# Fewer row-sum matmuls in the attention of a transformer layer: one running sum per head on the diagonal, both heads' maxima turned together, and a VectorE addition that joins two partial sums off the diagonal

## The chip, the cores and the metric

The kernel runs on one core of a Trainium2 chip. The metric is the time of one execution on the device in microseconds (us). The engines' names in the profile are PE (TensorE's matmuls), PEld (TensorE's weight loads), DVE (VectorE), ACT (ScalarE), POOL (GpSimd) and SP (SyncE, which issues transfers).

## The reference

One layer computes a layer norm, causal attention with 16 heads of 32 over 2048 tokens, and a gated feed-forward block, all in float32. Cut to what matters here:

```python
scores = jnp.einsum('bhqd,bhkd->bhqk', q, k) * scale
scores = jnp.where(causal, scores, jnp.finfo(scores.dtype).min)
probs = jax.nn.softmax(scores, axis=-1)
attn = jnp.einsum('bhqk,bhkd->bhqd', probs, v)
...
x = x + attn_out + ffn_out      # ffn: dequantised gate, up and down weights, tanh gelu
```

## The kernel before

Three stages follow one another: norm and projection (until about 160 us), attention (160 to 757 us), and output projection with feed-forward (757 us to the end). The change is in attention alone.

Attention goes through the 16 heads in 8 **pairs**. A pair has 40 **steps**: a step is one chunk of 512 queries against one tile of 128 keys. Four steps make a **group**, so a pair has 10 groups and the kernel has 80 (`NG`), with the index `k`. A group is **diagonal** if its keys are those of its own queries, and **full** otherwise; over the ten groups of a pair the order is D F D F F D F F F D (0 to 9), which makes 32 diagonal and 48 full groups. Each engine has its own program, and counting semaphores join them.

What each engine does for a group:

- **PE** computes the scores with keys on the partitions (`scores_t`, four steps ahead; with `mask_t` on the diagonal), and 8 **units** of scores with queries on the partitions (`scores`, line 772), which are used only for the row maxima and run up to 56 units ahead. It puts row maxima through a turning matmul (`turn_max`), multiplies exponentials and values (`product_v`, line 825), and adds up the exponentials over the keys with a matmul against a column of ones (`row_sums`, line 837). `row_sums(k)` of a diagonal group stands right behind its own products; that of a full group stands in the next group, behind seven of that group's eight units and ahead of its products. The eighth unit comes last in the group.
- **DVE** takes the maximum of each unit (`unit_max`, lines 697 and 701) in order. The units share a ring of four banks (`S_BUFS`), in which a turning also takes a slot.
- **ACT** takes the exponentials (line 638) into a ring of 16 tiles, `e_sb`, and copies turned maxima to `q_stack`.
- **POOL** adds exponentials in pairs of steps into `e_sum` (line 570), a ring of 6 tiles: four additions a group, two per head, each of two tiles. It also splits the row maxima into three parts (`split`) and multiplies the output of the pair before by its reciprocals (`normalise`, line 602, four times a pair).

The four matmuls of a quartet in `product_v` and `row_sums` write to four different quarters of the partitions (two heads, two halves of the queries), and their records overlap in time. A float32 matmul leaves two records, a bfloat16 or float32r matmul one.

DVE's loop over groups takes the units of a group with `for n in units: unit_max(n)`. The last units belong to group 72; groups 73 to 79 have none.

Of the kernel before, what the change touches and what calls it, by code (L numbers as in the profile page):

```python
# [292 lines left out]
def attention(nc, qk_scratch, v_scratch, sum_scratch, rsum_scratch, wo_t, wo_sb, attn_t, xn_hi, xn_lo, e_sb, wv_hi, wv_lo, p_v,  # L293
# [7 lines left out]
    HALF = W // 2  # L301
    SUMS = 4
    SUM_BUFS = 6
# [45 lines left out]
    for p in range(PAIRS):  # L349
        for r in range(TC):  # L350
            last = p * NU + UNITS_TO[r]
            BATCHES[-1 if last <= FIRST else next(k for k in range(NG) if unit_end[k] >= last)].append((p, r))
            wanted = (p * NS + CHUNK_START[r] - LEAD) // GS
            for a in range(2):
                TURNS[max(-1, -1 if p == 0 and r < 2 else wanted - TURN_LEAD)].append((p, r, a))
    turn_index = {}
# [12 lines left out]

    def summed(k, m):  # L370
        g = GS * k + 2 * (m // 2)
        q0, q1 = STEPS[g % NS][2], STEPS[(g + 1) % NS][2]
        return g * PIECES + m % 2, (g + 1) * PIECES + m % 2, q1 - q0, W - q1

    pool_sums = {(k, m): SUMS * k + m + 1 for k in range(NG) for m in range(SUMS)}

# [4 lines left out]
    with ExitStack() as ctx:  # L381
# [19 lines left out]
        rest2 = sb("rest2", [P, 2, TT], F32)  # L401
        max_cols = sb("max_cols", [P, 2, TT, D], BF16)
        ident = sb("ident_bf", [P, P], BF16)
# [25 lines left out]
        exp_done = sem("exp_done")  # L429
        pool_summed = sem("pool_summed")  # L430
        rows_done = sem("rows_done")
        pv_done = sem("pv_done")
# [103 lines left out]
        def _(pool):  # L536
# [22 lines left out]
            def sum_steps(k, part, before):  # L559
                for m in part:  # L560
                    if k < 0 or k >= NG:
                        continue
                    n = SUMS * k + m
                    x, y, skip, w = summed(k, m)
                    pool.wait_ge(exp_done, y + 1)
                    if before:
                        pool.wait_ge(normalised, before)
                    if n >= SUM_BUFS:
                        pool.wait_ge(rows_done, (n - SUM_BUFS) // SUMS + 1)
                    nc.gpsimd.tensor_tensor(e_sum[:, n % SUM_BUFS, 0:w], e_sb[:, x % E_BUFS, skip:skip + w],  # L570
                                            e_sb[:, y % E_BUFS, 0:w], ALU.add).then_inc(pool_summed, 1)

            def split(p, r, before):

                n = p * TC + r
                tiles = slice(4 * r, 4 * r + 4)
                pool.wait_ge(row_maxed, n + 1)
                if before:
                    pool.wait_ge(normalised, before)
                if p:  # L580
                    pool.wait_ge(max_turned, turn_index[p - 1, r, 1] + 1)
                nc.gpsimd.tensor_copy(max_cols[:, :, tiles, 0], row_max[:, :, tiles]).then_inc(split_step, 1)
                pool.wait_ge(split_step, 4 * n + 1)
                nc.gpsimd.tensor_tensor(rest1[:, :, tiles], row_max[:, :, tiles], max_cols[:, :, tiles, 0],
                                        ALU.subtract).then_inc(split_step, 1)
                pool.wait_ge(split_step, 4 * n + 2)
                nc.gpsimd.tensor_copy(max_cols[:, :, tiles, 1], rest1[:, :, tiles]).then_inc(split_step, 1)
                pool.wait_ge(split_step, 4 * n + 3)
                nc.gpsimd.tensor_tensor(rest2[:, :, tiles], rest1[:, :, tiles], max_cols[:, :, tiles, 1],
                                        ALU.subtract).then_inc(split_step, 1)  # L590
                pool.wait_ge(split_step, 4 * n + 4)
                nc.gpsimd.tensor_copy(max_cols[:, :, tiles, 2], rest2[:, :, tiles]).then_inc(max_split, 1)

# [12 lines left out]
            for k in range(-1, NG):  # L606
                sum_steps(k, (2, 3), products)
# [3 lines left out]
                sum_steps(k + 1, (0, 1), products)  # L611
                p, s = divmod(GS * k, NS)
                if p > 0 and s in (24, 28, 32, 36):
                    normalise(p - 1, products % TC, splits, pool_sums[min((k + 1, 1), (NG - 1, SUMS - 1))])
                    products += 1

        @block.scalar
        def _(act):
            def max_row(p, r, a):
                act.wait_ge(max_turned, turn_index[p, r, a] + 1)  # L620
                nc.scalar.activation(q_stack[p % PB][a][ROWS:P, r * W:(r + 1) * W],
                                     p_s[ROWS:P, slot[p, r, a] % S_BUFS, :], ACT.Copy).then_inc(max_rows, 1)

            def exps(x):
# [5 lines left out]
                if x >= E_BUFS:  # L630
                    old = piece(x - E_BUFS)[0]
                    j, i = divmod(old, GS)
                    act.wait_ge(pv_done, old + 1)
                    if DIAG[old % NS] and i % 2 == 0:
                        act.wait_ge(rows_done, j + 1)
                    m = 2 * (i // 2) + (x - E_BUFS) % PIECES
                    act.wait_ge(pool_summed, pool_sums[j, m])
                nc.scalar.activation(e_sb[:, x % E_BUFS, 0:w], bank_st(x)[:, 0:w], ACT.Exp,  # L638
# [46 lines left out]
        def _(dve):  # L685
# [30 lines left out]
            def divide(qc):  # L716
# [13 lines left out]
                for a in range(2):  # L730
                    for h in range(2):
                        rows = slice((2 * a + h) * D, (2 * a + h + 1) * D)
                        nc.vector.tensor_tensor(attn_rows(p, a, qc)[:, h * HALF:(h + 1) * HALF], o[rows, 0, :],
                                                recip[rows, 0:HALF], ALU.mult).then_inc(divided, 1)

            for n in range(FIRST):
                unit_max(n)
                for p, r in BATCHES[-1]:
                    if n + 1 == UNITS_TO[r]:
                        join_parts(p, r)  # L740
            for k in range(NG):
                p, s = divmod(GS * k, NS)
                if p and s == 16:
                    invert_sums(p - 1)
                units = units_of(k)
                for n in units:
                    unit_max(n)
                    for p_, r in BATCHES[k]:
                        if n + 1 == p_ * NU + UNITS_TO[r]:
                            join_parts(p_, r)  # L750
# [5 lines left out]
        def _(pe):  # L756
            def bank_free(n):

                before = ring[n - S_BUFS] if n >= S_BUFS else None
                if before in turn_index:  # L760
                    pe.wait_ge(max_rows, turn_index[before] + 1)
                elif before is not None:
                    pe.wait_ge(maxed, before + 1)
# [11 lines left out]

            def turn_max(p, r, a):

                n = slot[p, r, a]
                pe.wait_ge(max_split, p * TC + r + 1)
                bank_free(n)  # L780
                for t in range(W // P):
                    last = nc.tensor.matmul(p_s[ROWS:P, n % S_BUFS, t * P:(t + 1) * P],
                                            max_cols[:, a, 4 * r + t, :], ident[:, :], start=True, stop=True)
                last.then_inc(max_turned, 1)

            def scores_t(x):
# [6 lines left out]
                if kt == 0:  # L793
                    pe.wait_ge(max_rows, turn_index[p, qc, a] + 1)
                if x >= ST_BUFS:
# [35 lines left out]
            def row_sums(k):  # L831
                p, s = divmod(GS * k, NS)
                pe.wait_ge(pool_summed, pool_sums[k, SUMS - 1])


                def add(a, h, first, end, what, stop):
                    return nc.tensor.matmul(p_o[(2 * a + h) * D:(2 * a + h + 1) * D, 1, first:end], ones[:, :], what,  # L837
                                            start=False, stop=stop)

                if DIAG[s]:  # L840
                    for a in range(2):
                        x, _, _, _ = summed(k, a)
                        add(a, 0, 0, P, e_sb[:, x % E_BUFS, 0:P], False)
                    for a in range(2):
                        n = SUMS * k + a
                        add(a, 0, P, HALF, e_sum[:, n % SUM_BUFS, 0:P], True)
                    for a in range(2):
                        n = SUMS * k + a
                        add(a, 1, 0, HALF, e_sum[:, n % SUM_BUFS, P:3 * P], False)
                    for a in range(2):  # L850
                        x, _, _, _ = summed(k, 2 + a)
                        add(a, 1, 0, P, e_sb[:, x % E_BUFS, 0:P], False)
                    for a in range(2):
                        n = SUMS * k + 2 + a
                        last = add(a, 1, P, HALF, e_sum[:, n % SUM_BUFS, 0:P], True)
                else:
                    for j in range(2):
                        for h in range(2):
                            for a in range(2):
# [460 lines left out]
```

## Time and profile before

| | |
|---|---|
| median of 3 runs | 1872.63 us (1871.89 to 1872.90) |
| the profiled execution's own time | 1872.51 us |
| its span | 1870.6 us |
| PE busy over the span | 1815.5 us, 97% |
| DVE, ACT, POOL busy over the span | 59%, 38%, 37% |
| PE busy in attention, 160 to 757 us | 578.54 us of 597 |
| DVE, ACT, POOL busy in attention | 373.10, 347.56, 397.74 us |

An engine's busy time is the union of its instructions' records. A row of a timeline begins with the start and the duration in us, merges equal neighbours (xcount), and in brackets names the idle time ahead of it and what ended it; of a merged row, start plus duration is the end of the last record. PEclk is the granted clock of TensorE: 1.00 is 2.4 GHz and 0.50 is 1.2 GHz.

### The profile page before, as it was taken

The numbers are of one execution on the slowest core, as the hardware profiler recorded it, in microseconds if no ns is written. First come the engines' busy times: TensorE is split into PE (matmuls) and PEld (weight loads), VectorE is DVE, ScalarE is ACT, GpSimd is POOL, SyncE is SP. The second block draws the span as 40 slices with busy tenths as digits, with TensorE's granted clock in tenths as the row PEclk, the third lists the DMA queues.
The fourth block names the chain that finished last, engine by engine and source line by source line (L and its number), as shares of the span: only waits on it lengthen the run. The fifth ranks groups of instructions, "written<-read, shape, count | busy, mean of one in ns | idle before, by whom it ended". The sixth has DMA issues, their size and how long they took to land.

```text
span 1870.6 us, 29693 instructions
## 1 busy us (share of the span) xinstructions
PE 1815.5 (97%) x10880; PEld 1372.9 (73%) x10880; DVE 1111.8 (59%) x1695; ACT 698.5 (37%) x1144; POOL 702.7 (38%) x674
## 2 busy tenths in 40 slices
PE   6999999999999999899999999999999999999997
PEld 4877666666666664368888888888888888888886
DVE  4514766666666665437756665676666567666642
ACT  2313565665655655013332233232322333223221
POOL 4330567677677677112222222222222222222221
PEclk9999999999999999999999999999999999999999
DMA  7675041341341400521001101100110110010002
GB/s 247 218 213 156 27 89 42 79 89 39 81 89 35 85 8 13 213 68 34 7 28 34 34 0 34 34 13 21 34 34 0 34 34 18 16 34 0 0 1 90
DMA packets 73011, 108.64 MB, mean 58 GB/s; under 512 B 24608, under 2 KB 44688, under 8 KB 69264
## 3 DMA queue, kind: packets, MB, share of 16 engines
q1 hardware_dynamic: 72912, 107.34, 21.0%
q8 instruction: 59, 0.97, 0.2%
q14 instruction: 40, 0.33, 0.1%
HBM read 74.04 MB, written 29.59 MB: 55 GB/s over the span
## 4 chain that ended last, share of the span: by engine, by line
PE 58%; DVE 0%; ACT 0%; POOLq 0%; issue 0%; POOL 0%
PE p_gate L50 6%; PE p_gate L51 6%; PE p_gate L49 6%; PE p_out L49 6%; PE p_out L50 6%; PE p_out L51 6%; PE p_up L50 6%; PE p_up L51 6%; PE p_up L49 6%; PE p_out L1248 1%; PE p_gate L1248 1%; PE p_up L1248 1%; DVE acc L1183 0%; POOLq L939 0%; DVE inter L1163 0%
## 5 line engine op out<-in xcount | busy, mean ns | idle before, releaser
L1107 POOL TENSOR_SCALAR poly<-poly 128x1024 f32<-128x1024 f32 x64 | 71.3, 1113 | 839.5 <-ACT poly L1074 839.5
L570 POOL TENSOR_TENSOR e_sum<-e_sb 128x512 f32<-128x512 f32 (+2 forms) x320 | 331.3, 1063 | 107.5 <-PE p_o L837 103.8
L701 DVE TENSOR_REDUCE max_part<-p_s 128x1 f32<-128x512 f32 x384 | 240.8, 683 | 57.0 <-PE p_s L772 56.4
L638 ACT ACTIVATE e_sb<-p_v 128x512 f32<-128x512 f32 (+3 forms) x427 | 216.3, 552 | 142.4 <-PE p_v L799 76.6
L1163 DVE SCALAR_TENSOR_TENSOR inter<-inter,gate 128x1024 f32<-128x1024 f32 x64 | 78.4, 1225 | 255.2 <-ACT inter L1079 254.5
L772 PE MATMUL p_s<-k_stack,q_stack 96*128 96x512 f32 (+3 forms) x640 | 217.2, 393 | 3.7 <-DMA k_stack<-qk_scratch 3.2
L697 DVE CUSTOM_DVE_ANT_0 recip<-p_s,score_mask 128x128 bf16<-128x128 f32 (+3 forms) x256 | 119.7, 487 | 166.3 <-PE p_s L772 163.9
L49 PE MATMUL p_out<-i_hi,w_hi 128*128 128x512 f32 x512 | 200.0, 391 | 3.1 <-DVE acc L1183 3.1
L50 PE MATMUL p_out<-i_lo,w_hi 128*128 128x512 f32 x512 | 199.7, 390 | 0.0
L51 PE MATMUL p_out<-i_hi,w_lo 128*128 128x512 f32 x512 | 199.7, 390 | 0.0
L49 PE MATMUL p_gate<-xn_hi,w_hi 128*128 128x512 f32 x512 | 199.6, 390 | 0.0
L51 PE MATMUL p_gate<-xn_hi,w_lo 128*128 128x512 f32 x512 | 199.2, 389 | 0.0
L50 PE MATMUL p_gate<-xn_lo,w_hi 128*128 128x512 f32 x512 | 199.2, 389 | 0.0
L49 PE MATMUL p_up<-xn_hi,w_hi 128*128 128x512 f32 x512 | 199.2, 389 | 0.0
L50 PE MATMUL p_up<-xn_lo,w_hi 128*128 128x512 f32 x512 | 199.2, 389 | 0.0
L51 PE MATMUL p_up<-xn_hi,w_lo 128*128 128x512 f32 x512 | 199.2, 389 | 0.0
L1073 ACT ACTIVATE gate<-p_gate 128x1024 f32<-128x1024 f32 x64 | 65.9, 1029 | 355.4 <-PE p_gate L51 355.4
L1110 POOL TENSOR_TENSOR poly<-poly,gate 128x1024 f32<-128x1024 f32 x64 | 178.3, 2785 | 5.3
L799 PE MATMUL p_v<-q_stack,k_stack 128*128 128x512 f32 (+3 forms) x427 | 159.3, 397 | 8.1 <-ACT e_sb L638 5.1
L825 PE MATMUL p_o<-e_sb,v_stack 128*32 128x256 f32 (+1 forms) x2304 | 152.8, 370 | 0.0
L1183 DVE TENSOR_TENSOR acc<-acc,p_out 128x2048 f32<-128x2048 f32 x64 | 145.9, 2280 | 7.4 <-PE p_out L51 7.4
L772 PEld LDWEIGHTS p_s<-k_stack,q_stack 96*128 96x128 f32 x640 | 116.1, 190 | 43.6 <-issue 23.6
(124 smaller groups left out, 3060.6 us busy)
## 6 DMA issues: line engine op xcount, KB each, us to landing
q_stack<-qk_scratch SPq DMA_DIRECT2D x48, 256.0 KB, 7.1
k_stack<-qk_scratch SPq DMA_DIRECT2D x48, 256.0 KB, 8.1
qk_scratch<-out_hi SPq DMA_DIRECT2D x32, 256.0 KB, 2.6
qk_scratch<-out_lo SPq DMA_DIRECT2D x32, 256.0 KB, 3.2
scales<-in_gate_up_s SPq DMA_DIRECT2D x128, 64.0 KB, 2.3
x_sb<-in_x SPq DMA_DIRECT2D x4, 1024.0 KB, 13.2
xn_lo_scratch<-xn_lo SPq DMA_DIRECT2D x4, 1024.0 KB, 5.2
v_scratch<-o_sb SPq DMA_DIRECT2D x16, 256.0 KB, 2.0
```

The costliest lines, as they stand in the source:

```text
L49: nc.tensor.matmul(out, w_hi, x_hi, start=first, stop=False)
L50: nc.tensor.matmul(out, w_hi, x_lo, start=False, stop=False)
L51: return nc.tensor.matmul(out, w_lo, x_hi, start=False, stop=last)
L570: nc.gpsimd.tensor_tensor(e_sum[:, n % SUM_BUFS, 0:w], e_sb[:, x % E_BUFS, skip:skip + w], e_sb[:, y % E_BUFS, 0:w], ALU.add).then_inc(poo ...
L638: nc.scalar.activation(e_sb[:, x % E_BUFS, 0:w], bank_st(x)[:, 0:w], ACT.Exp, scale=SCALE).then_inc(exp_done, 1)
L697: nc.vector.tensor_tensor_reduce(out=masked_scores[:, m % 2, 0:w], in0=p_s[:, slot[n] % S_BUFS, 0:w], in1=score_mask[:, W - w:], scale=1.0 ...
L701: nc.vector.reduce_max(part, p_s[:, slot[n] % S_BUFS, 0:w], AX.X).then_inc(maxed, 1)
L772: nc.tensor.matmul(p_s[:, slot[n] % S_BUFS, 0:w], q_stack[p % PB][a][0:ROWS, i * P:(i + 1) * P], k_stack[p % PB][a][0:ROWS, b * W:b * W + ...
L799: last = nc.tensor.matmul(bank_st(x)[:, 0:W - q0], k_stack[p % PB][a][:, kt * P:(kt + 1) * P], q_stack[p % PB][a][:, qc * W + q0:(qc + 1) ...
L825: last = nc.tensor.matmul(p_o[(2 * a + h) * D:(2 * a + h + 1) * D, 0, first - h * HALF:], v_stack[p % PB][:, kt, a, :], e_sb[:, (g * PIECE ...
L1110: nc.gpsimd.tensor_tensor(poly[:, :, :], poly[:, :, :], gate[:, :, :], ALU.mult).then_inc(poly_done, 1)
L1183: nc.vector.tensor_tensor(here, here, p_out[:, :, :], ALU.add).then_inc(added, 1)
```

## The change

Three things are changed.

1. **Diagonal groups.** Before, POOL made two sums per head (steps 0+1 and 2+3) and PE multiplied ten tiles by ones. Now POOL adds steps 2 and 3 in place to the sum of steps 0+1, so a group has six additions (2 of 384 columns, 2 of 256, 2 of 128) and PE has six matmuls.
2. **Full groups.** POOL's four additions stay. DVE then adds the second sum of a head to the first (`join_sums`, two additions of 128x512 a group), and PE has four matmuls of 256 columns in place of eight. `row_sums` of a full group waits for DVE now (`vector_summed`), no longer for POOL.
3. **Turned maxima.** `max_cols` holds the two heads side by side, and one turning of 64 rows takes the place of two of 32. It takes one slot of the ring; ACT copies both heads out of it with two instructions, as before.

```diff
+    ADDS, first_sum, sums, added = [], [], 0, 0
+    adds_before, sum_group = [], []
+    for k in range(NG):
+        if DIAG[GS * k % NS]:
+            ADDS.append([(a, a, 1, 0) for a in range(2)] + [(a, a, i, None) for i in (2, 3) for a in range(2)])
+        else:
+            ADDS.append([(2 * j + a, a, 2 * j + 1, 2 * j) for j in range(2) for a in range(2)])
...
+                    if x is None:
+                        here = e_sum[:, n % SUM_BUFS, q0 - P:W - P]
+                        pool.wait_ge(pool_summed, adds_before[k] + i - 1)
+                        other = here
...
+            def join_sums(k):
+                if k not in FULL:
+                    return
+                for a in range(2):
+                    one, other = ((first_sum[k] + m) % SUM_BUFS for m in (a, 2 + a))
+                    dve.wait_ge(pool_summed, adds_before[k] + 3 + a)
+                    nc.vector.tensor_tensor(e_sum[:, one, :], e_sum[:, one, :], e_sum[:, other, :],
+                                            ALU.add).then_inc(vector_summed, 1)
...
                 units = units_of(k)
+                if len(units) < 6:
+                    join_sums(k - 1)
                 for n in units:
                     unit_max(n)
+                    if len(units) >= 6 and n == units[5]:
+                        join_sums(k - 1)
...
                 for t in range(W // P):
-                    last = nc.tensor.matmul(p_s[ROWS:P, n % S_BUFS, t * P:(t + 1) * P],
-                                            max_cols[:, a, 4 * r + t, :], ident[:, :], start=True, stop=True)
+                    last = nc.tensor.matmul(p_s[2 * D:P, n % S_BUFS, t * P:(t + 1) * P],
+                                            max_cols[:, 4 * r + t, :, :].rearrange("p a d -> p (a d)"), ident[:, :],
+                                            start=True, stop=True)
...
             def row_sums(k):
                 p, s = divmod(GS * k, NS)
-                pe.wait_ge(pool_summed, pool_sums[k, SUMS - 1])
+                if DIAG[s]:
+                    pe.wait_ge(pool_summed, adds_before[k] + len(ADDS[k]))
+                else:
+                    pe.wait_ge(vector_summed, 2 * FULL.index(k) + 2)
...
-                    for j in range(2):
-                        for h in range(2):
-                            for a in range(2):
-                                n = SUMS * k + 2 * j + a
-                                last = add(a, h, 0, HALF, e_sum[:, n % SUM_BUFS, h * HALF:(h + 1) * HALF], False)
+                    for h in range(2):
+                        for a in range(2):
+                            last = add(a, h, 0, HALF, total(a, h * HALF, (h + 1) * HALF), False)
```

The order on DVE around group 8 of the first pair, before. L697 and L701 are the maxima of units (an `ISA` row of `max_part` alone is the second half of a masked maximum), L708 joins their parts:

```order
L697 ISA recip,max_part<-p_s,score_mask 128x384 [waits maxed,scored]
L697 ISA max_part 128x1
L697 ISA recip,max_part<-p_s,score_mask 128x384 [waits maxed,scored]
L697 ISA max_part 128x1
L701 TENSOR_REDUCE max_part<-p_s 128x1 [waits scored] x4
L697 ISA recip,max_part<-p_s,score_mask 128x512 [waits maxed,scored]
```

The same place in the changed kernel (L722 and L726 are the unit maxima there):

```order
L722 ISA recip,max_part<-p_s,score_mask 128x384 [waits maxed,scored]
L722 ISA max_part 128x1
L722 ISA recip,max_part<-p_s,score_mask 128x384 [waits maxed,scored]
L722 ISA max_part 128x1
L726 TENSOR_REDUCE max_part<-p_s 128x1 [waits scored] x4
L767 TENSOR_TENSOR e_sum<-e_sum 128x512 [waits pool_summed] x2
L722 ISA recip,max_part<-p_s,score_mask 128x512 [waits maxed,scored]
```

The two additions of the group before stand behind the maxima of six units and ahead of those of the seventh and eighth.

The order on PE at the end of the same group, before: seventh unit (L772), two turnings (L782), row sums of the group before (L837), products (L825):

```order
L772 MATMUL p_s<-k_stack,q_stack 128x512 [waits maxed]
L782 MATMUL p_s<-ident_bf,max_cols 32x128 [waits maxed,max_split]
L782 MATMUL p_s<-ident_bf,max_cols 32x128 x3
L782 MATMUL p_s<-ident_bf,max_cols 32x128 [waits maxed,max_split]
L782 MATMUL p_s<-ident_bf,max_cols 32x128 x3
L837 MATMUL p_o<-e_sum,ones 32x256 [waits pool_summed]
L837 MATMUL p_o<-e_sum,ones 32x256 x7
L825 MATMUL p_o<-e_sb,v_stack 32x256 [waits exp_done]
```

The same place on PE in the changed kernel (L810 unit, L820 turning, L879 row sums, L864 products):

```order
L810 MATMUL p_s<-k_stack,q_stack 128x512 [waits maxed]
L820 MATMUL p_s<-ident_bf,max_cols 64x128 [waits maxed,max_split]
L820 MATMUL p_s<-ident_bf,max_cols 64x128 x3
L879 MATMUL p_o<-e_sum,ones 32x256 [waits vector_summed]
L879 MATMUL p_o<-e_sum,ones 32x256 x3
L864 MATMUL p_o<-e_sb,v_stack 32x256 [waits exp_done]
```

Half of the turnings and half of the row sums are gone; the row sums keep their place, and the semaphore ahead of them is another.

## Rows read from the trace of the kernel before

**Rows 1.** Busy time by engine in attention (windows).

```profile
core 0: us, PE busy (x) PEld busy (x) DVE busy (x) ACT busy (x) POOL busy (x), PEclk, DMA share, GB/s
160.00:757.00 597.00, 578.54 (x5559) 372.82 (x5557) 373.10 (x926) 347.56 (x757) 397.74 (x503) 0.99 0.28 61
```

**Rows 2.** Timeline of PE: turnings, row sums of a full group, products.

```profile
399.83 0.59 PE L782 MATMUL p_s<-ident_bf,max_cols 128*32 128x128 bf16 x5
400.21 0.42 PE L837 MATMUL p_o<-e_sum,ones 128*32 128x256 f32 x3
...
401.10 1.26 PE L825 MATMUL p_o<-e_sb,v_stack 128*32 128x256 f32 x17
```

**Rows 3.** Timeline of PE: end of the row sums of diagonal group 30.

```profile
410.06 0.39 PE L837 MATMUL p_o<-e_sb,ones 128*32 128x128 f32 x4
410.28 0.39 PE L837 MATMUL p_o<-e_sum,ones 128*32 128x128 f32 x4
```

**Rows 4.** Timeline of DVE: maxima up to a sixth unit (groups 32, 34, 35, 37, 38, 39).

```profile
418.78 3.68 DVE L701 TENSOR_REDUCE max_part<-p_s 128x1 f32<-128x512 f32 x6 [0.37 <-PE p_s L772]
...
434.59 1.29 DVE L701 TENSOR_REDUCE max_part<-p_s 128x1 f32<-128x512 f32 x2 [0.39 <-PE p_s L772]
...
441.88 1.28 DVE L701 TENSOR_REDUCE max_part<-p_s 128x1 f32<-128x512 f32 x2
...
455.31 1.88 DVE L701 TENSOR_REDUCE max_part<-p_s 128x1 f32<-128x512 f32 x3
...
461.00 2.62 DVE L701 TENSOR_REDUCE max_part<-p_s 128x1 f32<-128x512 f32 x4
...
467.65 3.68 DVE L701 TENSOR_REDUCE max_part<-p_s 128x1 f32<-128x512 f32 x6
```

**Rows 5.** Timeline of PE: start of the row sums in the same six groups.

```profile
421.40 1.07 PE L837 MATMUL p_o<-e_sum,ones 128*32 128x256 f32 x16
...
435.48 0.42 PE L837 MATMUL p_o<-e_sum,ones 128*32 128x256 f32 x3
...
442.26 1.07 PE L837 MATMUL p_o<-e_sum,ones 128*32 128x256 f32 x16
...
455.95 1.07 PE L837 MATMUL p_o<-e_sum,ones 128*32 128x256 f32 x16
...
463.33 0.42 PE L837 MATMUL p_o<-e_sum,ones 128*32 128x256 f32 x3
...
470.90 0.42 PE L837 MATMUL p_o<-e_sum,ones 128*32 128x256 f32 x3
```

**Rows 6.** Groups by form, DVE: an operation of two SBUF operands, 128x512.

```profile
L1139 DVE TENSOR_TENSOR pair<-pair,high 128x512 int32<-128x512 int32 x48 | 33.2, 692 | 1.6
```

**Rows 7.** Line 733: durations min/median/max, first and last start.

```profile
L733 DVE TENSOR_TENSOR acc<-o_sb,recip x12: 419/1383/1541, 710.4 to 735.4; 32x256 f32<-32x256 f32 x12
L733 DVE TENSOR_TENSOR acc<-p_o,recip x4: 416/422/430, 755.3 to 756.7; 32x256 f32<-32x256 f32 x4
```

**Rows 8.** Timeline of POOL: normalise in groups 37 and 39.

```profile
456.29 1.28 POOL L602 TENSOR_TENSOR acc<-acc,rsum_rows 64x512 f32<-64x512 f32 x1 [0.23 <-POOL e_sum L570]
...
471.22 1.28 POOL L602 TENSOR_TENSOR acc<-acc,rsum_rows 64x512 f32<-64x512 f32 x1 [0.23 <-POOL e_sum L570]
```

**Rows 9.** Waits over the span: us in total, times, longest.

```profile
POOL e_sum L570 <- PE p_o L837: 103.8, 43, 7.4
```

**Rows 10.** POOL's additions of 384 columns (lines), the last two of 128 (timeline).

```profile
L570 POOL TENSOR_TENSOR e_sum<-e_sb 128x384 f32<-128x384 f32 x64 | 63.1, 1006 | 0.1
...
751.47 0.86 POOL L570 TENSOR_TENSOR e_sum<-e_sb 128x128 f32<-128x128 f32 x2
```

**Rows 11.** PE and its granted clock in three stretches (windows), one timeline row.

```profile
176.90:180.30 3.40, 2.66 (x19) 1.00 0.40 154
...
740.00:743.50 3.50, 2.67 (x19) 1.00 0.00 0
743.50:746.90 3.40, 3.40 (x36) 0.50 0.00 0
...
743.39 1.85 PE L837 MATMUL p_o<-e_sum,ones 128*32 128x256 f32 x16
```

More of the change, by code:

```diff
@@ L353, in attention @@
             wanted = (p * NS + CHUNK_START[r] - LEAD) // GS
-            for a in range(2):
-                TURNS[max(-1, -1 if p == 0 and r < 2 else wanted - TURN_LEAD)].append((p, r, a))
+            TURNS[max(-1, -1 if p == 0 and r < 2 else wanted - TURN_LEAD)].append((p, r))
     turn_index = {}
@@ L366, in attention, with used_up @@
     slot = {what: n for n, what in enumerate(ring)}
[L370 to L375, printed above, removed]
+    ADDS, first_sum, sums, added = [], [], 0, 0
[5 more added lines that the diff above has]
+            ADDS.append([(2 * j + a, a, 2 * j + 1, 2 * j) for j in range(2) for a in range(2)])
+        first_sum.append(sums)
+        adds_before.append(added)
+        sum_group += [k] * (2 if DIAG[GS * k % NS] else 4)
+        sums = len(sum_group)
+        added += len(ADDS[k])
+    FULL = [k for k in range(NG) if not DIAG[GS * k % NS]]
+    def used_up(g, a):
+        k, i = divmod(g, GS)
+        return adds_before[k] + 1 + max(n for n, (_, b, y, x) in enumerate(ADDS[k]) if b == a and i in (x, y))
     def piece(x):
@@ L430, in attention @@
         pool_summed = sem("pool_summed")
+        vector_summed = sem("vector_summed")
         rows_done = sem("rows_done")
@@ L559, in sum_steps @@
             def sum_steps(k, part, before):
[L560 to L565, printed above, removed]
+                if k < 0 or k >= NG:
+                    return
+                for i, (m, a, y, x) in list(enumerate(ADDS[k]))[part]:
+                    n = first_sum[k] + m
+                    g = GS * k + y
+                    q0 = STEPS[g % NS][2]
+                    here = e_sum[:, n % SUM_BUFS, 0:W - q0]
+                    pool.wait_ge(exp_done, g * PIECES + a + 1)
                     if before:
                         pool.wait_ge(normalised, before)
[L568 to L571, printed above, removed]
+                    if x is None:
[3 more added lines that the diff above has]
+                    else:
+                        if n >= SUM_BUFS:
+                            pool.wait_ge(rows_done, sum_group[n - SUM_BUFS] + 1)
+                        skip = q0 - STEPS[(GS * k + x) % NS][2]
+                        other = e_sb[:, ((GS * k + x) * PIECES + a) % E_BUFS, skip:skip + W - q0]
+                    nc.gpsimd.tensor_tensor(here, other, e_sb[:, (g * PIECES + a) % E_BUFS, 0:W - q0],
+                                            ALU.add).then_inc(pool_summed, 1)
             def split(p, r, before):
@@ L606, in _ @@
             for k in range(-1, NG):
-                sum_steps(k, (2, 3), products)
+                sum_steps(k, slice(2, None), products)
                 for p, r in BATCHES[k]:
@@ L610, in _ @@
                     splits += 1
-                sum_steps(k + 1, (0, 1), products)
+                sum_steps(k + 1, slice(0, 2), products)
                 p, s = divmod(GS * k, NS)
                 if p > 0 and s in (24, 28, 32, 36):
-                    normalise(p - 1, products % TC, splits, pool_sums[min((k + 1, 1), (NG - 1, SUMS - 1))])
+                    normalise(p - 1, products % TC, splits, adds_before[k + 1] + 2 if k + 1 < NG else added)
                     products += 1
@@ L618, in _, with max_row @@
         def _(act):
[L619 to L622, printed above, removed]
+            def max_row(p, r):
+                act.wait_ge(max_turned, turn_index[p, r] + 1)
+                for a in range(2):
+                    nc.scalar.activation(q_stack[p % PB][a][ROWS:P, r * W:(r + 1) * W],
+                                         p_s[(2 + a) * D:(3 + a) * D, slot[p, r] % S_BUFS, :],
+                                         ACT.Copy).then_inc(max_rows, 1)
             def exps(x):
@@ L631, in exps @@
                     old = piece(x - E_BUFS)[0]
-                    j, i = divmod(old, GS)
                     act.wait_ge(pv_done, old + 1)
[L634 to L637, printed above, removed]
+                    act.wait_ge(pool_summed, used_up(old, (x - E_BUFS) % PIECES))
+                    if STEPS[old % NS][1] == 4 * STEPS[old % NS][0]:
+                        act.wait_ge(rows_done, old // GS + 1)
                 nc.scalar.activation(e_sb[:, x % E_BUFS, 0:w], bank_st(x)[:, 0:w], ACT.Exp,
@@ L760, in bank_free @@
                 if before in turn_index:
-                    pe.wait_ge(max_rows, turn_index[before] + 1)
+                    pe.wait_ge(max_rows, 2 * turn_index[before] + 2)
                 elif before is not None:
@@ L774, in scores, with turn_max @@
                                  ).then_inc(scored, 1)
-            def turn_max(p, r, a):
-                n = slot[p, r, a]
+            def turn_max(p, r):
+                n = slot[p, r]
                 pe.wait_ge(max_split, p * TC + r + 1)
@@ L793, in scores_t @@
                 if kt == 0:
[L794 removed]
+                    pe.wait_ge(max_rows, 2 * turn_index[p, qc] + a + 1)
                 if x >= ST_BUFS:
@@ L838, in add, with total @@
                                             start=False, stop=stop)
+                def total(m, first, end):
+                    return e_sum[:, (first_sum[k] + m) % SUM_BUFS, first:end]
                 if DIAG[s]:
                     for a in range(2):
-                        x, _, _, _ = summed(k, a)
-                        add(a, 0, 0, P, e_sb[:, x % E_BUFS, 0:P], False)
+                        add(a, 0, 0, P, e_sb[:, (GS * k * PIECES + a) % E_BUFS, 0:P], False)
                     for a in range(2):
-                        n = SUMS * k + a
-                        add(a, 0, P, HALF, e_sum[:, n % SUM_BUFS, 0:P], True)
+                        add(a, 0, P, HALF, total(a, 0, P), True)
                     for a in range(2):
[L848 to L855, printed above, removed]
-                else:
-                    for j in range(2):
-                        for h in range(2):
-                            for a in range(2):
-                                n = SUMS * k + 2 * j + a
-                                last = add(a, h, 0, HALF, e_sum[:, n % SUM_BUFS, h * HALF:(h + 1) * HALF], False)
+                        last = add(a, 1, 0, HALF, total(a, P, 3 * P), True)
+                else:
+                    for h in range(2):
+                        for a in range(2):
+                            last = add(a, h, 0, HALF, total(a, h * HALF, (h + 1) * HALF), False)
                 last.then_inc(rows_done, 1)
```

21 lines of the change are left out of this document (11 added, 10 removed).

## The prediction

> **What bounds the kernel now.** I read the busy times of attention first. PE is busy for 578.54 of 597 us there, DVE for 373.10 and POOL for 397.74 [rows 1]: PE sets the pace, and on an average over the stage the others have room. That invites the sum "fewer matmuls, less time". But PE runs its program in order, so I then read, group by group, at what moment DVE has finished the sixth unit and at what moment PE reaches the row sums [rows 4, 5]. There is no room at that place: DVE is still behind PE there.
>
> **What the change takes from PE.** Row sums of a full group: eight matmuls take from 400.21 to the first product at 401.10, 0.89 us [rows 2], so four cost 0.445 and 48 groups give 48 x 0.445 = 21.4 us. Diagonal groups: of the second half's matmuls, two sets of 128 columns go; a set takes 410.28 - 410.06 = 0.22 us [rows 3], so 0.44 a group and 32 x 0.44 = 14.1 us. The first half loses nothing. Turnings: eight matmuls start within 0.38 us (399.83 to 400.21) [rows 2]; four fewer save 0.2. This counts only in the one turning of four per pair behind which no full group's row sums stand; in the other three PE only arrives earlier at a wait (below). 8 x 0.2 = 1.6 us. Together 37.1 us.
>
> **What it puts on the path.** PE's row sums of full group k-1 now need both additions on DVE, and these stand in DVE's order behind the sixth unit of group k. The sixth unit ends, in the six groups of one pair that follow a full one, at 422.46, 435.88, 443.16, 456.59, 463.62 and 471.33 (start plus duration; in group 37 the merged row holds the fifth to seventh units, so one unit of 0.60 less) [rows 4]. PE starts the row sums at 421.40, 435.48, 442.26, 455.95, 463.33 and 470.90 [rows 5]. So DVE is 1.06, 0.40, 0.90, 0.64, 0.29 and 0.43 us late before it has added anything, 3.7 us a pair.
>
> The addition itself (128x512 float32, both operands in SBUF) isn't in this trace. The nearest row has the same shape, both operands in SBUF and four bytes an element: 692 ns [rows 6]. Two are 1.38 us. From below, the mean unit maximum costs about 0.61 from start to start (3.68 us for six), so two are at least 1.2; from above see "collisions". I take 1.38 because the row differs only in the operation. The stall is then 3.7 + 6 x 1.38 = 12.0 us a pair.
>
> I count it in full. DVE's chain starts when PE has scored a group's first unit, and it sets when the row sums start; behind them PE still has the products, the eighth unit and the next group's first scores before it can score another first unit. While PE waits, nothing of that gets done, since it is queued behind the waiting matmul. Only PE's savings behind the wait come off, and they are in the 37.1. Seven pairs and group 72 (1.06 + 1.38 = 2.4) make 43 such waits: 7 x 12.0 + 2.4 = 86.4 us. In groups 73 to 79 DVE has no units and joins early, so there I add nothing.
>
> **Collisions of DVE and POOL.** A DVE multiplication of 32x256 takes 422 ns with one operand in PSUM while POOL is idle, and 1383 ns (median) with both in SBUF while POOL adds [rows 7]: DVE waits there until POOL's current instruction has ended. So I looked where POOL is when the joins would start. In groups 37 and 39 it is in a normalisation that ends at 457.57 and 472.50 [rows 8], 0.98 and 1.17 us behind DVE's sixth unit: 2.15 a pair, 7 x 2.15 = 15.0 us. In the other four POOL is mostly idle. Over the span it waits for PE's row sums 43 times, 2.4 us each [rows 9], and the joins fall just ahead of those row sums. Bounds: nothing, and one such wait for each of two additions in all 43 groups, 43 x 2 x (1.383 - 0.422) = 83 us.
> The Trainium skill (SBUF — State Buffer, "SBUF: two separate sides") has a rule against this change: VectorE with two SBUF inputs and GpSimd share a port pair under an exclusive lock, and the one that comes second is blocked for the whole instruction. By it a join that meets POOL pays what is left of POOL's instruction, and every meeting costs; line 733's times agree, and what it doesn't say is how often they meet.
>
> **POOL's extra work.** Two more additions of 256 columns in a diagonal group, each between 0.455 (128 columns, 0.86 for two) and 1.006 us (384) [rows 10], say 0.73: 1.46 a group. They hide under a group of PE (597 us / 80 = 7.5 us), and the diagonal sums no longer need a slot freed by the group before. In group 79 nothing hides them: POOL's last addition ends at 752.33 [rows 10], PE's last row sums stand behind it, and 1.5 us are added. Splitting into another layout and ACT's copies keep their number and size: nothing.
>
> **The clock.** In 740.0 to 743.5 PE was busy for 2.67 of 3.5 us in short pieces, and the next 3.4 us ran at 0.50, that is at 1.2 GHz [rows 11]. Eight row-sum matmuls took 1.85 us there against 1.07 in group 37 [rows 5, 11], 0.78 more; a stretch of 3.4 us at half speed loses at most 1.7. Against it: with 2.66 of 3.4 us busy at 176.9 the clock stood at 1.00 [rows 11], and over the whole stage it is 0.99 [rows 1]. The new waits are 2 us on average and in one piece, more idle time than either case. I take a fall behind half of the 43 waits at 1.2 us, midway: 26 us. Bounds: none, and 43 x 1.7 = 73 us.
> The Trainium skill (TensorE: Matmul & The Clock Gate, "HAM oscillation") tells of kernels in which every wait is followed by a cold start. By that rule the term would be its upper bound, and the time 1938 + 73 = 2011 us.
>
> **The sum**, against the profiled execution's 1872.5 us (0.1 below the median of the runs shown): -37.1 + 86.4 + 15.0 + 1.5 = +65.8 gives 1938.3; with the clock's 26 it is 1964.
>
> **The rivals.**
>
> - *The waits come, the clock holds*: 1922 without any collision (1872.5 - 37.1 + 86.4) to 1938 with those above. For it: the full clock at 176.9. Chance 0.30.
> - *The clock falls behind every wait, or POOL meets every join*: 2011, or 1922 + 83 + 1.5 = 2006. For it: the waits are long, and line 733 shows how dear a meeting is. Against it: POOL's 43 idle times. Chance 0.14.
> - *The other side: the joins hide* and PE keeps its saving: 1872.5 - 37.1 + 1.5 = 1837. It takes two finished additions when PE arrives, that is DVE earlier by 1.67 to 2.44 us in each group (lateness plus 1.38). It would happen if DVE could start units earlier than now; each of the six chains starts when PE scores its first unit, so I see no way. It decides from the point where the stall per pair is under 37.1/7.2 = 5.2 us in place of 12.0. Chance 0.05.
> - *Saving and waits cancel*, within 0.2% (3.7 us): the stall a pair would have to be half of what I read. Chance 0.02.
>
> **How the numbers follow.** My forecast (waits, some collisions, clock falling behind some of the waits; 1940 to 2000) has 0.49 and is centred on 1964. The range must hold 8 in 10: 1914 (the first rival's low end with additions at 1.2 a pair of them, 43 x 0.18 = 7.7 less) to 2008 (the second rival's two prices). What a measurement of this kernel can tell from no change is about 0.2%. Faster by more: 0.05; within: 0.02; slower by more: 0.93.
>
> **What would show it.** In the new profile PE idles ahead of the row sums, released by DVE's `e_sum` additions, 43 times by about 2 us, and attention is longer by 40 us at least, while the stages around it keep their times. Six units and two additions stand on DVE without a gap ahead of each such release. The additions take about 0.69 us, 1 us more where they meet POOL. PEclk within attention shows falls to 0.50 if the last term is right. PE's busy time falls by some 37 us if the clock holds. I'm wrong if the additions start ahead of the sixth unit's end, or if PE's waits are shorter than 1 us; then the saving shows.

## The result, and the profile after

The changed kernel takes 1998.8 us (median of 4 runs, 1996.29 to 2001.54) against 1872.26 us: 1.0678 times the time of before, 95% interval 1.0662 to 1.0693. The profiled execution took 1996.29 us, 123.8 more than that of before. The forecast was 1964 with a range of 1914 to 2008.

First the stretches. Windows of the changed kernel, attention and what follows it (busy time of each engine, granted clock):

```profile
160.00:885.00 725.00, 604.31 (x4785) 360.42 (x4784) 457.00 (x1016) 350.13 (x754) 449.67 (x567) 0.90 0.22 50
885.00:1994.50 1109.50, 1099.48 (x4732) 889.14 (x4730) 678.01 (x648) 309.09 (x304) 249.58 (x128) 1.00 0.11 33
```

All of the loss is in attention: it ends at about 881 us, not 757, and the rest of the program takes as long as before. PE's busy share there fell from 97% [rows 1] to 83%, and its mean granted clock from 0.99 to 0.90. PE has fewer matmuls and yet more busy time (604 us against 578.54), because some of them ran at half speed.

Then the waits over the whole span (us in total, times, longest):

```profile
PE p_o L879 <- DVE e_sum L767: 102.2, 46, 3.3
POOL e_sum L593 <- PE p_o L879: 61.5, 24, 5.2
```

L879 are the row sums, L767 is the new addition. PE waits 46 times, 2.2 us each; the wait didn't exist before. POOL waits for PE's row sums for 61.5 us in place of 103.8 [rows 9].

The new addition's line (durations in ns, minimum, median, maximum):

```profile
L767 DVE TENSOR_TENSOR e_sum<-e_sum x96: 677/682/1790, 206.8 to 869.8; 128x512 f32<-128x512 f32 x96
```

The timeline of group 37, the one that stood in [rows 4, 5, 8]. DVE:

```profile
505.95 0.42 DVE L722 CUSTOM_DVE_ANT_0 recip<-p_s,score_mask 128x256 bf16<-128x256 f32 x1
506.29 1.28 DVE L726 TENSOR_REDUCE max_part<-p_s 128x1 f32<-128x512 f32 x2
507.49 2.20 DVE L767 TENSOR_TENSOR e_sum<-e_sum 128x512 f32<-128x512 f32 x2
509.62 0.68 DVE L726 TENSOR_REDUCE max_part<-p_s 128x1 f32<-128x512 f32 x1
514.12 0.69 DVE L726 TENSOR_REDUCE max_part<-p_s 128x1 f32<-128x512 f32 x1 [3.82 <-PE p_s L810]
```

PE and POOL in the same group:

```profile
506.60 0.39 PE L838 MATMUL p_st<-q_stack,k_stack 128*128 128x512 f32 x1
509.75 1.08 PE L879 MATMUL p_o<-e_sum,ones 128*32 128x256 f32 x8 [2.76 <-DVE e_sum L767]
510.60 3.05 PE L864 MATMUL p_o<-e_sb,v_stack 128*32 128x256 f32 x32
...
507.29 1.26 POOL L627 TENSOR_TENSOR acc<-acc,rsum_rows 64x512 f32<-64x512 f32 x1 [0.23 <-POOL e_sum L593]
```

Read it in this order. DVE runs six units without a gap and then the two additions; they take 2.20 us in place of 1.28, because the first meets POOL's normalisation, which ends at 508.55. PE has nothing left to do from about 507.0 and starts its row sums at 509.75, right behind the additions. Then its products take 3.05 us for 32 records: at full speed they took 1.91 (456.84 to 458.75 in the trace of before). The windows of PE say why:

```profile
507.00:510.40 3.40, 0.65 (x8) 0.87 0.00 0
509.50:512.90 3.40, 3.15 (x32) 0.50 0.00 0
512.90:516.00 3.10, 3.10 (x29) 1.00 0.00 0
```

Behind the wait the clock is granted at 0.50 (1.2 GHz), and the products run in that stretch.

Not every wait is followed by such a fall. In group 27, the same place one pair earlier, PE waited almost as long, and its products ran at full speed (timeline of PE):

```profile
422.67 0.64 PE L879 MATMUL p_o<-e_sum,ones 128*32 128x256 f32 x8 [2.58 <-DVE e_sum L767]
423.13 1.91 PE L864 MATMUL p_o<-e_sb,v_stack 128*32 128x256 f32 x32
```

By the timeline of PE and its windows, the clock was at 0.50 over part of what followed in 36 of the 46 waits; behind the other ten the products took the full-speed 1.91 us for 32 records, or 1.70 for 24.

### The profile page after: what moved, and what is told of

Read it like the earlier page. It is cut to its first block, busy times and chain, and to the rows that moved or that the text cites. A ratio compares the mean times of both kernels' runs of the same rounds, so it can differ in the third digit from the quotient of the medians.

```text
span 1994.5 us, 28287 instructions
## 1 busy us (share of the span) xinstructions
PE 1840.8 (92%) x10112; PEld 1361.4 (68%) x10112; DVE 1197.7 (60%) x1791; ACT 701.8 (35%) x1144; POOL 754.7 (38%) x738
## 4 chain that ended last, share of the span: by engine, by line
PE 55%; DVE 0%; ACT 0%; POOLq 0%; issue 0%; POOL 0%
PE p_gate L49 6%; PE p_gate L51 6%; PE p_gate L50 6%; PE p_out L49 6%; PE p_out L50 6%; PE p_out L51 6%; PE p_up L49 6%; PE p_up L50 6%; PE p_up L51 6%; PE p_out L1282 1%; PE p_gate L1282 1%; PE p_up L1282 1%; DVE acc L1217 0%; POOLq L973 0%; DVE inter L1197 0%
## 5 line engine op out<-in xcount | busy, mean ns | idle before, releaser
L593 POOL TENSOR_TENSOR e_sum<-e_sb 128x512 f32<-128x512 f32 (+1 forms) x256 | 306.5, 1225 | 75.3 <-PE p_o L879 61.5
L726 DVE TENSOR_REDUCE max_part<-p_s 128x1 f32<-128x512 f32 x384 | 241.2, 682 | 69.5 <-PE p_s L810 69.0
L722 DVE CUSTOM_DVE_ANT_0 recip<-p_s,score_mask 128x128 bf16<-128x128 f32 (+3 forms) x256 | 119.5, 486 | 200.6 <-PE p_s L810 198.1
L810 PE MATMUL p_s<-k_stack,q_stack 96*128 96x512 f32 (+3 forms) x640 | 219.9, 397 | 1.0 <-DMA k_stack<-qk_scratch 0.4
L864 PE MATMUL p_o<-e_sb,v_stack 128*32 128x256 f32 (+1 forms) x2304 | 189.4, 441 | 0.0
L879 PE MATMUL p_o<-e_sum,ones 128*32 128x256 f32 (+1 forms) x640 | 82.6, 470 | 102.2 <-DVE e_sum L767 102.2
L663 ACT ACTIVATE e_sb<-p_st 128x512 f32<-128x512 f32 (+2 forms) x213 | 117.6, 552 | 116.5 <-PE p_st L838 72.9
```

What stands on the lines that cost most here:

```text
L593: nc.gpsimd.tensor_tensor(here, other, e_sb[:, (g * PIECES + a) % E_BUFS, 0:W - q0], ALU.add).then_inc(pool_summed, 1)
L722: nc.vector.tensor_tensor_reduce(out=masked_scores[:, m % 2, 0:w], in0=p_s[:, slot[n] % S_BUFS, 0:w], in1=score_mask[:, W - w:], scale=1.0 ...
L726: nc.vector.reduce_max(part, p_s[:, slot[n] % S_BUFS, 0:w], AX.X).then_inc(maxed, 1)
L810: nc.tensor.matmul(p_s[:, slot[n] % S_BUFS, 0:w], q_stack[p % PB][a][0:ROWS, i * P:(i + 1) * P], k_stack[p % PB][a][0:ROWS, b * W:b * W + ...
L864: last = nc.tensor.matmul(p_o[(2 * a + h) * D:(2 * a + h + 1) * D, 0, first - h * HALF:], v_stack[p % PB][:, kt, a, :], e_sb[:, (g * PIECE ...
```

## The experiments

The kernel before was measured beside each set of these kernels, at 1871.6 to 1872.0 us. Group and pair are those of the front part.

**One change taken out: no joining on DVE.** Full groups have their eight row-sum matmuls again; diagonal sums and joint turning stay.

```diff
-                    pe.wait_ge(vector_summed, 2 * FULL.index(k) + 2)
+                    pe.wait_ge(pool_summed, adds_before[k] + len(ADDS[k]))
...
-                if len(units) < 6:
-                    join_sums(k - 1)
```

> The diagonal sums and the joint turning alone: full groups keep their four POOL sums and eight row-sum matmuls of before, and DVE joins nothing. My theory, by which the cost comes from PE waiting for DVE's additions: 1872.3 less 14.1 us (diagonal row sums) and less 32 x 0.2 = 6.4 us (turnings, which all count now), plus 1.5 us at the end: about 1853 us, and PEclk in attention back at 0.99. The rival, by which POOL's two extra additions in a diagonal group or the changed ring of sums slow the kernel: above 1872 us, with PE waiting for POOL's e_sum in diagonal groups.

Measured: 1863.25 us, ratio 0.9958 (0.9944 to 0.9972). The loss is gone, and the sign of the theory holds: the joining, with the four row-sum matmuls a group that it saves, turns 1863 into 1999. But the gain is 8.6 us, not 19. Waits of this kernel:

```profile
PE p_o L875 <- POOL e_sum L593: 13.1, 8, 3.2
```

Six of these waits stand at the end of a pair, 8.9 us together, where PE needs POOL's in-place additions. They are those of the second to the seventh pair; at the end of the first, which has no normalisations, PE doesn't wait. The other two, 4.2 us, belong to the last pair, where the kernel before has one of 1.8 us as well. The timeline of POOL and then of PE at the end of a pair (group 39):

```profile
460.60 1.95 POOL L593 TENSOR_TENSOR e_sum<-e_sb 128x384 f32<-128x384 f32 x2
462.78 1.28 POOL L627 TENSOR_TENSOR acc<-acc,rsum_rows 64x512 f32<-64x512 f32 x1 [0.23 <-POOL e_sum L593]
464.19 2.23 POOL L593 TENSOR_TENSOR e_sum<-e_sum,e_sb 128x256 f32<-128x256 f32 x4
...
466.48 0.30 PE L875 MATMUL p_o<-e_sb,ones 128*32 128x128 f32 x2 [1.47 <-POOL e_sum L593]
```

The four additions take 2.23 us, two of them new, behind a normalisation; PE waits 1.47 us for the last. So 20.5 us saved as reckoned, less the 11.3 us of waits that are new (13.1 less 1.8), are 9.2; measured 8.6.

**The wait is kept, the clock is held.** Zeros are multiplied ahead of PE's wait, in the groups that have units (`FILL` is 4):

```diff
                 if k and not DIAG[GS * (k - 1) % NS]:
+                    if units:
+                        for _ in range(FILL):
+                            for h in range(2):
+                                for a in range(2):
+                                    nc.tensor.matmul(p_o[(2 * a + h) * D:(2 * a + h + 1) * D, 1, 0:HALF], score_mask[:, 0:D],
+                                                     score_mask[:, 0:HALF], start=False, stop=False)
                     row_sums(k - 1)
```

> The changed kernel with work added that changes nothing in the result: ahead of PE's wait for DVE's additions, 16 matmuls of 256 columns of zeros (four quartets, 4 x 0.445 = 1.8 us) in each of the 43 groups that have units. The DVE chain stays as it is. If the fall of TensorE's clock behind the waits is worth some 50 us of the 127, added work makes the kernel faster: 1940 to 1960 us, with nearly no stretch at 0.50 in attention. The rival, by which the whole loss is the wait itself and the collisions: no faster than 1998.8 us, up to 10 us slower where the filler outlasts the wait.

Measured: 1942.34 us, ratio 1.0373 (1.0356 to 1.0390). With 688 matmuls more the kernel is 56.5 us faster than the changed one. The line of the zeros among PE's lines (busy time, mean ns of a record; matmuls leave two records each):

```profile
L948 PE MATMUL p_o<-score_mask 128*32 128x256 f32 x1376 | 83.2, 382 | 0.0
```

The windows of this kernel's attention:

```profile
160.00:830.00 670.00, 622.65 (x6165) 378.59 (x6164) 460.06 (x1021) 350.33 (x754) 449.15 (x567) 0.99 0.24 54
```

The clock is back at 0.99, and PE still waits for DVE, for the rest (waits):

```profile
PE p_o L880 <- DVE e_sum L768: 27.2, 31, 2.7
```

So the fall of the clock costs 56.5 us at least, and the wait with all else at most 70.5 (1942.3 less 1871.85). The split isn't exact, because the zeros outlast the waits: 83.2 us of zeros and 27.2 of waits are left where there were 102.2 of waits, 8.2 more. By that estimate the clock is worth up to 56.5 + 8.2 = 64.7 us.

**The wait is moved on PE: row sums behind the products.**

```diff
-                if k and not DIAG[GS * (k - 1) % NS]:
-                    row_sums(k - 1)
                 for g in range(GS * k, GS * k + GS):
                     product_v(g)
+                if k and not DIAG[GS * (k - 1) % NS]:
+                    row_sums(k - 1)
```

> The changed kernel with one step moved on PE: the row sums of a full group stand behind the next group's products in place of ahead of them. DVE's additions, their collisions with POOL and all counts stay. My theory, the place of the wait: products of about 1.7 us now lie beside DVE's chain of six units and two additions, so the stall falls from 2 to 3 us to between 0.3 and 1.2 us, the clock mostly holds, and the time is 1850 to 1890 us. POOL gets its slots in the ring of sums 1.7 us later, which may bring back some waits of ACT. The rival, by which the additions themselves and their meetings with POOL are dear wherever they are waited for: 1960 us or more.

Measured: 1915.05 us, ratio 1.0226 (1.0208 to 1.0243). 84 us of the loss go with one step moved, so most of it isn't the additions as such but where they are waited for. It is 25 us above what I expected, however. Waits of this kernel:

```profile
PE p_o L879 <- DVE e_sum L767: 40.4, 33, 3.2
PE p_o L879 <- POOL e_sum L593: 16.0, 9, 4.1
```

One of the nine in the timeline of PE:

```profile
566.15 0.30 PE L879 MATMUL p_o<-e_sb,ones 128*32 128x128 f32 x2 [1.45 <-POOL e_sum L593]
```

PE waits for DVE 102.2 - 40.4 = 62 us less, and the 16.0 us for POOL were 1.7 in the changed kernel. An addition has a median of 1.1 us here and not 0.68. That it meets POOL more often is the likely reason; it wasn't followed up. The clock fell here too (0.980 over the span).

**The wait is moved on DVE: the additions behind the second unit** (`n == units[1]` in place of `units[5]`).

> The changed kernel with DVE's two additions behind the second unit in place of the sixth. PE then finds them done; but the ring of four banks makes PE wait for the maxima of the later units, which come 1.28 us and the collisions later: PE reaches the row sums when the third unit is cleared, some 0.5 to 1 us late in 43 groups. My theory, the place of the wait on DVE: 1865 to 1900 us. The rival, by which DVE's extra work sets the pace wherever it stands: within 10 us of 1998.8 us.

Measured: 1951.85 us, ratio 1.0424 (1.0407 to 1.0442). 47 us better, and 52 above the upper end of what I expected. PE hardly waits for DVE's sums any more (4.0 us in the last groups) but for a free bank of the ring, that is for the maxima that the additions have pushed back (waits):

```profile
PE p_s L810 <- DVE max_part L722: 33.2, 20, 2.3
PE p_s L810 <- DVE max_part L726: 24.1, 22, 2.2
PE p_o L879 <- POOL e_sum L593: 15.0, 9, 2.6
```

57.3 us in 42 waits, 1.4 each where I had reckoned 0.5 to 1, plus the clock (0.974 over the span, 0.993 with the filler) and POOL. The rival, "within 10 us of 1998.8", falls; so does my size.

**POOL's normalisations one group earlier**, on four kernels (`s in (20, 24, 28, 32)` in place of `(24, 28, 32, 36)`).

> Diagonal sums and joint turning alone, as in the first run, and the four normalisations of a pair one group earlier on POOL (groups 5 to 8 of a pair in place of 6 to 9). In that first run PE waited 8 times, 13.1 us together, for POOL's in-place additions of group 9, which stand on POOL behind a normalisation. My theory: with the normalisation out of group 9 most of these waits go, and the time falls from 1863.3 to about 1851 us. The rival: POOL is full over the whole run of full groups, so the waits stay or move, and the time stays within 3 us of 1863.

> Row sums of full groups behind the products (which measured 1915 us) and the normalisations one group earlier. There PE waited 1.5 to 7 us for POOL at the end of a pair and 0.9 to 1.9 us for DVE's additions. If the first is made by the normalisation behind which POOL's diagonal additions queue, 5 us a pair go: 1870 to 1885 us. If POOL is late because its slots in the ring of sums are freed later, the time stays within 10 us of 1915.

> The changed kernel with the normalisations one group earlier. The additions of DVE in group 9 met a normalisation and POOL's diagonal additions there (2.9 us for two in place of 1.28), and PE waited some 0.5 us for POOL behind it. My theory of collisions: 1.2 us of the additions and 0.5 us of the wait go in 8 pairs, and some of the clock's falls: 1975 to 1990 us. The rival, by which a join meets POOL's next instruction wherever that is: within 5 us of 1998.8.

> The control: the kernel before with only the normalisations one group earlier. PE waited there for POOL's e_sum for 6 us in all, so both theories expect 1869 to 1873 us; if it is faster than that, the gain of the other three runs is not the change's.

Measured: 1873.73 us without joining (10 above its partner), 1924.48 with the row sums behind (9 above), 2004.77 for the changed kernel (6 above) and 1876.64, ratio 1.0025 (1.0016 to 1.0035), for the control. All four results lie outside what my theory gave. One rival covers its result: that of the second kernel, within 10 us of 1915. The first is clear of its partner; of the second and third the intervals (1.0241 to 1.0290, 1.0690 to 1.0726) touch those of their partners, so these two are slower at the edge of the noise. For the control I had also misread the trace of before: PE waits there for POOL's `e_sum` once, 1.8 us, and not for 6 us.

In the kernel without joining PE's wait for POOL has grown:

```profile
PE p_o L875 <- POOL e_sum L593: 18.1, 8, 3.2
```

The edit took out the normalisation behind the diagonal additions and left the one ahead of them, and it put another at the start of a run in which POOL then is never idle: from 446.48 to 479.85 its instructions stand with no gap over 0.3 us. So POOL has no room there from group 6 of a pair to group 0 of the next, though in the kernel before it is busy for only 398 of 597 us over attention. The wait grew by 5.0 us and the time by 10; the granted clock also went from 0.994 to 0.989 over the span.

**The normalisations out of that run**, on four kernels: all four of a pair at one place, in group 1 of the second pair after; those of the seventh pair stay.

```diff
-                if p > 0 and s in (24, 28, 32, 36):
-                    normalise(p - 1, products % TC, splits, adds_before[k + 1] + 2 if k + 1 < NG else added)
-                    products += 1
+                due = [p - 2] * TC if p > 1 and s == 4 else [p - 1] if p == PAIRS - 1 and s in (24, 28, 32, 36) else []
+                for done in due:
+                    normalise(done, products % TC, splits, adds_before[k + 1] + 2 if k + 1 < NG else added)
+                    products += 1
```

> Diagonal sums and joint turning alone, and the normalisations of a pair moved out of the run of full groups altogether: all four stand on POOL in group 1 of the second pair after, where POOL waited 7.4 us for PE in the trace of before (only those of the seventh pair stay where they are). Moving them one group earlier had made things worse, which says that POOL has no free time from group 6 of a pair to group 0 of the next. My theory, POOL full there and nowhere else: PE's 13.1 us of waits for POOL go in six of eight pairs, 1863.3 falls to about 1853 us. The rival, by which the additional additions cost elsewhere: within 3 us of 1863.

Measured: 1855.31 us, ratio 0.9914 (0.9897 to 0.9930). This is the fastest version: diagonal sums and joint turning without the joining on DVE. Its waits:

```profile
PE p_o L876 <- POOL e_sum L593: 4.2, 2, 3.2
```

Two are left, of the last pair. So the normalisation behind which POOL's additions queued was the cause of the other six: 8.9 us of waits went, and 7.9 us of time.

> The control: the kernel before with the normalisations moved in the same way. PE waited there for POOL's e_sum for some 6 us in all, in the last pair above all, so 1867 to 1872 us.

Measured: 1870.40 us, ratio 0.9994 (0.9985 to 1.0004): the move is worth nothing that can be measured to the kernel before. It gives room that only POOL's additional work needs.

> Row sums of full groups behind the products (1915 us), and the normalisations moved out of the run of full groups. That kernel's pairs took 75.8 us, with one group of 12.6 us at each pair's end, in which PE waited for POOL's diagonal additions. If POOL's load there is the cause, 5 us a pair and some falls of the clock go: 1865 to 1885 us. If the late freeing of the ring of sums is, within 15 us of 1915.

Measured: 1896.05 us, ratio 1.0120 (1.0103 to 1.0136): 19 us better than without the move, and 11 above what I expected. So the rival, within 15 us of 1915, falls too, but only part of POOL's lateness came from the normalisations: at a pair's end PE waits 0.77 us for POOL in place of 1.45. Two kinds of waits remain in this kernel:

```profile
PE p_o L880 <- DVE e_sum L768: 31.9, 23, 3.2
PE p_o L880 <- POOL e_sum L593: 12.0, 9, 4.1
```

> The changed kernel with the normalisations moved out of the run of full groups. In groups 7 and 9 of a pair DVE's two additions took 2.2 and 2.9 us in place of 1.28, each time across a normalisation. My theory of collisions: 0.9 and about 1 us a pair go, with 0.5 us of waiting for POOL in group 0, and perhaps a fall of the clock: 2.4 x 6 = 14 us or more off 1998.8, so 1970 to 1985. The rival: an addition meets whatever POOL does next, and the time stays within 5 us of 1998.8.

Measured: 1978.31 us, ratio 1.0569 (1.0551 to 1.0586): 20.5 us better than the changed kernel, as expected; PE waits for DVE 93.3 us, 8.9 less, and the granted clock over the span is 0.967 in place of 0.959.

## Why the prediction was right

Its main mechanism held: PE waits for DVE's additions, it waits about as long as reckoned, and the clock falls behind the waits. Two small steps failed, and the sum was 35 us too low (1964 against 1998.8), nearly all of it by the size of one term, the clock. The time came out at the upper edge of the forecast of 1940 to 2000, nearer to the second rival (2006 to 2011) than to the centre. Point by point:

- **PE's saving of 37.1 us**: the part outside the joining (14.1 + 6.4 us when all turnings count) is borne out by the first experiment: 8.6 us measured and 11.3 us of new waits make 19.9. The 21.4 us of the full groups were not measured alone.
- **The wait, 3.7 us a pair and 1.38 for two additions**: In the groups with units PE waits 43 times, 97.3 us together (waits of 160 to 850 us); the sum had 86.4, and 15.0 for collisions, 101.4 together. Two additions that meet nobody take 1.28 us (518.44 to 519.72, group 38), so the nearest row was 0.1 too dear.
- **Collisions, 15 us in groups 37 and 39**: the right groups. In the timeline of DVE two additions take 2.20 us in the first and 2.91 in the second:

```profile
518.44 1.28 DVE L767 TENSOR_TENSOR e_sum<-e_sum 128x512 f32<-128x512 f32 x2
...
528.74 2.91 DVE L767 TENSOR_TENSOR e_sum<-e_sum 128x512 f32<-128x512 f32 x2
```

  That is 0.92 and 1.63 over 1.28, 2.55 in this pair where I had 2.15. In group 39 the second addition meets POOL's diagonal additions too, which I had not counted. What the Trainium skill says of the exclusive lock (SBUF — State Buffer, "SBUF: two separate sides") agrees with these rows.
- **POOL's extra work, 1.5 us in all**: this step was wrong. "They hide under a group of PE" holds for three diagonal groups of four; in the one at a pair's end they cost 1.5 us in six pairs of eight (8.9 us in the first experiment). In the changed kernel it hardly shows: PE waits for POOL's sums twice there, 1.7 us together. That its longer groups give POOL time is my reading and wasn't tested. I had compared POOL's work with a mean group, and the place has a run of full groups with normalisations ahead of it.
- **The last groups, "I add nothing"**: wrong too, by 4.9 us. PE waits for DVE's additions three more times, in groups without units (0.83, 2.78 and 1.29 us). DVE has its divisions there, and two of the three pairs of additions queue behind them; ahead of the third DVE itself waits for POOL.
- **The clock, 26 us**: the term that was mis-sized. It measured 56.5 us (filler against none; up to 64.7 by the estimate above), inside the bounds of 0 and 73 that I gave and nearer to the upper one. I had let it fall behind half of the waits at 1.2 us; it fell behind 36 of 46, and 56.5 / 36 are 1.6 us each. Both halves of the term were too small. The mean of 0.90 over 725 us means about 2 x 0.10 x 725 = 145 us at half speed, which could lose 73 us if it were full of work. What the Trainium skill tells of kernels in which every wait is followed by a cold start (TensorE: Matmul & The Clock Gate, "HAM oscillation") was closer than my half, though it didn't hold for ten of the 46 waits. The page's own case has waits of about 3 to 5 us; here waits of 1.37 us were followed by falls, and one of 2.58 was not.
- The sum without the clock was 1938.3; the kernel whose clock is held takes 1942.3. So the other terms were right to 4 us together. In part that is luck, since the waits, 4 us below the sum's figure, and the last groups, 4.9 us above it, cancel.

Open: how much of the 1896 us of the version with late row sums is DVE's wait and how much the clock, which was not held there; why one wait is followed by a fall of the clock and another of the same length is not; and whether the joining could pay with more banks in the ring or more slots for sums. That wasn't tried.

## What to carry to other kernels

An engine with a third of its time free can still be late at one place. Before putting work on it, read from the trace when it finishes the instruction behind which the new one will stand, and when its consumer gets there; the difference is paid each time, however free the engine is on average. An idle gap on TensorE may cost twice, once as itself and once in the clock of the matmuls behind it, and zeros multiplied into an accumulator tell the two apart. And when work is moved off a busy stretch of an engine, look where the stretch begins: a move of one place within it made no kernel faster (two were slower clear of the noise, two at its edge), a move out of it made the best one.

## What the runs showed of the hardware

- Added matmuls made the kernel faster: 688 matmuls of zeros, 56.5 us less, with the granted clock of attention at 0.99 in place of 0.90.
- Of 46 waits of TensorE inside a busy stage, of 0.83 to 3.3 us, 36 were followed by a granted clock of 0.50, some of them only 1.37 us long.
- Two SBUF operands on DVE against POOL: an addition of 128x512 float32 takes 0.68 us alone and up to 1.79 us when it meets a POOL addition; POOL's own four additions take 2.97 us there, against 2.23 us without a join (first experiment). The timeline of POOL in the changed kernel, group 39:

```profile
530.10 2.97 POOL L593 TENSOR_TENSOR e_sum<-e_sum,e_sb 128x256 f32<-128x256 f32 x4
```
